# Selective scan with feed-forward: the decay of the GpSimd-made steps moves from PSUM to the SBUF ring

## The reference

```python
dt = jax.nn.softplus(jnp.einsum('blr,dr->bld', x_dbl[..., :DT_RANK], dt_w) + dt_b)
A = -jnp.exp(A_log)
dA = jnp.exp(dt[..., None] * A)
dBu = dt[..., None] * Bm[:, :, None, :] * u[..., None]

def step(h, ins):
    dA_t, dBu_t, C_t = ins
    h = dA_t * h + dBu_t
    y = jnp.einsum('bdn,bn->bd', h, C_t)
    return (h, y)
```

## Time and profile before

| | us |
|---|---|
| median of 3 runs | 493.03 |
| lowest and highest run | 490.91, 496.62 |
| the profiled execution's own time | 496.12 |
| its span | 494.3 |

### The profile page before, as it was taken

The page is one execution under the profiler, slowest core; times in us unless marked ns, Lnnn a source line. Parts: engine busy times, 40 slices in busy tenths (PEclk is TensorE's granted clock), DMA queues, the critical chain, the costliest instruction groups (busy, mean ns, idle before and its releaser), DMA issues. The chain is left out here.

```text
span 494.3 us, 6553 instructions
## 1 busy us (share of the span) xinstructions
PE 410.5 (83%) x2200; PEld 276.7 (56%) x2200; DVE 422.3 (85%) x345; ACT 369.4 (75%) x719; POOL 404.3 (82%) x241
## 2 busy tenths in 40 slices
PE   1947995998699987989898998889998967798854
PEld 0335554664556574555655684555665845457643
DVE  3577997999989998988999879998999989899254
ACT  2298699679966969897889689898789786972040
POOL 1799689797988799988979899989899999958431
PEclk9967999998879998998999899999999895989778
DMA  8251242322241233222232314223322332210001
GB/s 238 87 196 46 86 110 82 110 85 91 64 146 47 90 108 107 86 91 65 85 108 100 112 50 107 86 92 106 108 86 107 79 106 93 70 42 2 0 1 42
DMA packets 17009, 43.48 MB, mean 88 GB/s; under 512 B 1616, under 2 KB 5968, under 8 KB 16976
## 3 DMA queue, kind: packets, MB, share of 16 engines
q1 hardware_dynamic: 16976, 43.06, 27.1%
HBM read 41.48 MB, written 1.57 MB: 87 GB/s over the span
## 5 line engine op out<-in xcount | busy, mean ns | idle before, releaser
L1020 POOL TENSOR_TENSOR hq<-hq,c_tiles 128x1024 f32<-128x1024 f32 x129 | 300.6, 2348 | 45.2 <-DVE hq L1147 42.7
L1147 DVE TENSOR_TENSOR_SCAN hq<-da,bb 128x1024 f32<-128x1024 f32 x113 | 255.9, 2280 | 10.0 <-PE bb L631 2.6
L650 PE MATMUL ysum<-wts,hq 128*128 128x128 f32 x1024 | 150.7, 295 | 18.5 <-POOL hq L1020 17.0
L816 ACT ACTIVATE da<-dt,neg_a 128x511 f32<-128x511 f32 x226 | 147.1, 711 | 7.1 <-DVE hq L1147 6.8
L650 PEld LDWEIGHTS ysum<-wts,hq 128*128 128x128 f32 x1024 | 122.9, 150 | 43.0 <-POOL hq L1020 24.3
L1128 DVE TENSOR_TENSOR bb<-bb,dtu 128x1024 f32<-128x1024 f32 x80 | 97.0, 1213 | 9.3 <-PE bb L604 5.8
L914 ACT ACTIVATE g<-dtu_t,bc_t 128x256 f32<-128x256 f32 x132 | 55.9, 497 | 0.0
L1147 DVE TENSOR_TENSOR_SCAN hq<-bb,dbu 128x1024 f32<-128x1024 f32 x15 | 34.3, 2286 | 13.4 <-ACT bb L827 6.3
L631 PE MATMUL bb<-wts,g 128*128 128x128 f32 x264 | 37.8, 290 | 9.1 <-ACT g L914 7.1
L631 PEld LDWEIGHTS bb<-wts,g 128*128 128x128 f32 x264 | 32.2, 150 | 18.5 <-issue 9.9
L604 PE MATMUL bb<-b_rows,pick 48*128 48x512 bf16 x76 | 30.4, 400 | 9.6 <-DVE hq L1147 9.6
(11 more groups left out here) (127 smaller groups left out, 500.1 us busy)
## 6 DMA issues: line engine op xcount, KB each, us to landing
c_tiles<-bc_rows_dram SPq DMA_DIRECT2D x64, 512.0 KB, 3.6
b_tiles<-bc_rows_dram SPq DMA_DIRECT2D x15, 256.0 KB, 4.4
wconv<-conv_taps_dram SPq DMA_DIRECT2D x2, 512.0 KB, 7.1
x_res<-x_dram SPq DMA_DIRECT2D x1, 768.0 KB, 9.2
out_dram<-o SPq DMA_DIRECT2D x3, 256.0 KB, 2.3
wts<-packed_dram SPq DMA_DIRECT2D x1, 584.0 KB, 10.2
hid<-w_ffn_dram SPq DMA_DIRECT2D x1, 576.0 KB, 8.6
bc_rows_dram<-xdbl SPq DMA_DIRECT2D x8, 64.0 KB, 3.1
```

Source lines behind the costliest of these rows:

```text
L650: mm = nc.tensor.matmul(ysum[:, h, block(b)], hq[:, i % H_RING, h, block(b)], ident, start=(first and b == 0), stop=(i % NS == NS - 1), is ...
L816: ins = nc.scalar.activation(da[:, i % DA_RING, h, 1:SEQ], dt[:, k % 2, h, 1:SEQ], ACT.Exp, scale=neg_a[:, c:c + 1])
L1020: nc.gpsimd.tensor_tensor(hq[:, i % H_RING, halves, :], hq[:, i % H_RING, halves, :], c_tiles[:, n % C_RING, i % 2, :].unsqueeze(1).broadc ...
L1147: nc.vector.tensor_tensor_scan(out=hq[:, i % H_RING].rearrange("p h t -> p (h t)"), data0=decay.rearrange("p h t -> p (h t)"), data1=dbu_t ...
```

## The change

The pooled steps' decay is made like all others, by `exp` into the ring `da`, some five steps ahead. The stage `exp_psum`, its semaphore and its copy of zeros are gone. The pooled scan reads `da` and `dbu`. The bank of `bb` that belongs to a pooled step stays untouched, so the step two later waits for the last scan that did use the bank (`last_in_bank`), which is four before it.

```diff
+def last_in_bank(i):
+
+    return max(n for n in range(i % BB_RING, i, BB_RING) if not is_pooled(n))
...
-        return [("exp", n) for n in ahead.get(i, (i + DA_RING - 1,)) if n < STEPS and not is_pooled(n)]
+        return [("exp", n) for n in ahead.get(i, (i + DA_RING - 1,)) if n < STEPS]
...
-            if i >= 1 and i + 1 < STEPS:
-                order.append(("g_turn" if is_turned(i + 1) else "exp_psum" if is_pooled(i + 1) else "bcast", i + 1))
+            if i >= 1 and i + 1 < STEPS and not is_pooled(i + 1):
+                order.append(("g_turn" if is_turned(i + 1) else "bcast", i + 1))
...
                     if i >= BB_RING:
-                        pe.wait_ge(s_scan, i - BB_RING + 1)
+                        pe.wait_ge(s_scan, last_in_bank(i) + 1)
...
-                elif stage == "exp_psum":
-
-                    i, = a
-                    k, n = i // NS, i % NS
-                    act.wait_ge(s_scan, i - BB_RING + 1)
-                    nc.scalar.activation(bb[:, i % BB_RING, :, 0:1], da[:, 0, :, 0:1], ACT.Copy)
-                    for h in range(2):
-                        c = (2 * (k % 2) + h) * NS + n
-                        ins = nc.scalar.activation(bb[:, i % BB_RING, h, 1:SEQ], dt[:, k % 2, h, 1:SEQ],
-                                                   ACT.Exp, scale=neg_a[:, c:c + 1])
-                    ins.then_inc(s_exp_psum, 1)
...
                     i, = a
+                    dve.wait_ge(s_exp, i + 1)
                     if is_pooled(i):
                         dve.wait_ge(s_dbu_pooled, pooled_steps(i) + 1)
-                        dve.wait_ge(s_exp_psum, pooled_steps(i) + 1)
+                    elif is_turned(i):
+                        dve.wait_ge(s_g_turn, turned_steps(i) + 1)
                     else:
...
-                    decay, dbu_tile = da[:, i % DA_RING], bb[:, i % BB_RING]
-                    if is_pooled(i):
-                        decay, dbu_tile = bb[:, i % BB_RING], dbu
+                    dbu_tile = dbu if is_pooled(i) else bb[:, i % BB_RING]
                     nc.vector.tensor_tensor_scan(out=hq[:, i % H_RING].rearrange("p h t -> p (h t)"),
-                                                 data0=decay.rearrange("p h t -> p (h t)"),
+                                                 data0=da[:, i % DA_RING].rearrange("p h t -> p (h t)"),
                                                  data1=dbu_tile.rearrange("p h t -> p (h t)"), initial=0.0,
```

More of the change, by code:

```diff
@@ L405, in mamba_sandwich @@
         s_exp = sem("da_done")
-        s_exp_psum = sem("da_in_psum_done")
         s_bl = [sem(f"b_tile{n}_loaded") for n in range(POOLED_RING)]
@@ L1132, in _ @@
                     i, = a
+                    dve.wait_ge(s_exp, i + 1)
                     if is_pooled(i):
                         dve.wait_ge(s_dbu_pooled, pooled_steps(i) + 1)
-                        dve.wait_ge(s_exp_psum, pooled_steps(i) + 1)
-                    else:
[L1137 to L1141, removed]
+                    elif is_turned(i):
+                        dve.wait_ge(s_g_turn, turned_steps(i) + 1)
+                    else:
+                        dve.wait_ge(s_dbu, plain_steps(i) + 1)
                     if i >= H_RING:
                         dve.wait_ge(s_fold, i - H_RING + 1)
-                    decay, dbu_tile = da[:, i % DA_RING], bb[:, i % BB_RING]
-                    if is_pooled(i):
-                        decay, dbu_tile = bb[:, i % BB_RING], dbu
+                    dbu_tile = dbu if is_pooled(i) else bb[:, i % BB_RING]
                     nc.vector.tensor_tensor_scan(out=hq[:, i % H_RING].rearrange("p h t -> p (h t)"),
-                                                 data0=decay.rearrange("p h t -> p (h t)"),
+                                                 data0=da[:, i % DA_RING].rearrange("p h t -> p (h t)"),
                                                  data1=dbu_tile.rearrange("p h t -> p (h t)"), initial=0.0,
```

## The result

| | before | changed |
|---|---|---|
| median, us | 494.82 (4 runs) | 509.61 (4 runs) |
| lowest and highest, us | 490.91, 496.89 | 509.15, 510.46 |
| ratio, 95% interval | | 1.031 (1.024 to 1.039) |
| span of the profiled execution, us | 494.3 | 508.7 |

The change made the kernel slower by 14.8 us between the medians. Of the kernel before's 17 executions there, the nine slow ones, more than 1.5% above its fastest, are left out of its median, 492.21 us, and of the ratio, as are eight of 17 beside the other experiments, where its median is 492.55. The difference is +18.7.

The account below looks back on a forecast made before the run. VectorE and GpSimd, both wanting nearly the whole unit, were taken to bound the kernel. Exclusion +14.4, fewer TensorE waits -2.1 and uncovered GpSimd time +1.0 gave +13.3 on 493.0: 506.3 us, range 490 to 518.

Parts of the forecast that it names:

- Exclusion, both ways: Pooled scans with two SBUF inputs and GpSimd operations exclude each other, first come first served; +6 to +22.3 us, chance 0.58.
- The sum over fifteen places: Waits of pooled scans for running GpSimd products, earlier-decay gains included: 5.7 at step 8 plus 8.6 at step 15, +14.4 us.
- Second order: Knock-on effects on VectorE's waits for TensorE and on GpSimd's spare time: -2.1 and +1.0 us.
- waits on TensorE that shrink: A later VectorE waits less for TensorE's broadcasts and turned products: a quarter of 8.4 us, -2.1.
- GpSimd's debt: GpSimd stands still during pooled scans, and its spare time in a unit leaves about 1 us uncovered: +1.0.
- Base: Sum applies to the profiled execution, 496.12 us, 3.1 above the median of the runs; forecast starts from 493.0.
- The earlier decay in front of the Silu: ScalarE's step 8 decay pair precedes the convolution's Silu, hidden by 13.4 us of TensorE waits; counted nothing, at most 9.9 us.
- The earlier release of the bank: Broadcast or turned product two steps after a pooled one no longer waits for its scan; counted nothing, at most 2.0 us.
- GpSimd keeping the port: Rival: GpSimd holds the port across back-to-back instructions; +22.5 us, 515.5 (508 to 524), chance 0.14.
- Only GpSimd waits: Rival: the pooled scan on VectorE never waits; about +1 us, 494 (487 to 501), chance 0.12.
- No exclusion for a scan: Rival: pooled scans overlap GpSimd products undisturbed, so half the earlier starts is kept; -6 us, 487 (481 to 493), chance 0.12.
- Waits that vanish in slack: Rival: VectorE's delays are real but fall into waits on TensorE and tail order; 490 to 497 us, chance 0.04.

Follow-up runs that it names:

- the small kernel: Separate kernel without the reference's computation: eight stages of four VectorE and GpSimd operations, alone or together; two-SBUF scans beside products 17.35 us, scans with one PSUM operand 9.35.
- the kernel with the PSUM operand: Changed kernel, but pooled scans read old values from PSUM as second operand and release the bank as before; 485.15 us, 0.985 of the kernel before.
- the two attempts with a sooner decay: Kernel before with the late decay one slot sooner, operands unchanged: at both steps 490.93 us, ratio 0.999; at step 15 alone 492.39, ratio 1.002.
- the kernel with step 15 alone: The change made only at step 15 of a unit (8 places), step 8 keeping its late decay in PSUM; 514.32 us, 1.046 of the kernel before.
- the small kernel's fifth stage: Stage of the separate two-engine kernel: four VectorE products of two SBUF tiles beside four GpSimd products; 13.40 us.

## Why the prediction was right

The forecast was 506.3 (490 to 518) and slower; measured were 509.6 and +14.8 against +13.3 forecast.

**Exclusion, both ways.** This was taken from one GpSimd instruction of 1.70 us and extended to VectorE without a row. The 4.09 to 4.38 us of eleven pooled scans and the stages of the small kernel show both directions.

**The sum over fifteen places.** Forecast 5.7 at step 8 and 8.6 at step 15. In the changed trace the seven scans at step 8 last 25.1 us instead of 16.0 with 5.3 less idle time before them: +3.9. The eight at step 15 last 32.8 instead of 18.3, less 6.0: +8.5. Together +12.4 of 14.4. The part at step 8 was too large by 1.8. At six of its seven places each turn is shorter than I took it, by about 0.1 (a scan that has waited ends 2.15 us after the product, not 2.29). The seventh, the last unit's, makes 1.3 of the 1.8: I counted +0.07 there, and the trace has -1.2, the scan lasting 2.87 instead of 2.29 us without the 1.79 of idle time before it. GpSimd was behind there and still at the product of step 6 (443.70 to 446.05), so the pooled scan waited for the rest of that one and not for the product of scan 7, which ended at 444.85.

**Second order.** I had -2.1 for waits on TensorE that shrink and +1.0 for GpSimd's debt. Neither is seen in that form: VectorE's other idle time between first and last scan is 23.1 us against 22.6, so nothing was absorbed, and its waits for broadcasts and turned products grew from 8.4 to 9.6. The term that I missed is the end. At the last unit's step 15 I counted -0.01, because the scan would start first. It did; but then the product of the step before waits for it, and nothing after it hides that. Two pieces of the chain of waits at the end, of the kernel before and of the changed one (start, us, what):

```profile
453.59 2.35 POOL hq L1020
...
456.41 2.35 POOL hq L1020
```

```profile
466.42 2.36 POOL hq L1013
...
469.24 4.25 POOL hq L1013
```

The product before the last one lasts 4.25 us on the chain instead of 2.35. From the end of the last scan to the end of the span it was 35.8 us and is 37.3. The balance of the spans closes: +0.45 before the first scan, +12.38 between, +1.55 behind, 14.38. That the forecast of the size came so near is in part luck: step 8 was 1.8 too large, and the end, which I had at nothing, gave nearly as much back; the two terms of the second order, -1.1 together, have nothing that answers to them.

**Base.** I had put the profiled execution 3.1 above the median; with the four runs of each it is 1.3 above, so of the 3.3 us between forecast and median 1.8 are the base and 1.5 the size.

**What was costed at nothing.** The earlier decay in front of the Silu: the Silus wait 9.0 us for TensorE instead of 13.4, and the kernel with the PSUM operand, which has the same order on ScalarE, is faster than before. The earlier release of the bank: the turned products waited 2.0 us for scans before and 0.9 in the changed kernel, no more than I bounded.

**The rivals.** GpSimd keeping the port: refuted by the turns. Only GpSimd waits: refuted by the scans' durations. No exclusion for a scan: refuted; the gain I gave it, -6, is near the 7.4 of the kernel without exclusion. Waits that vanish in slack: refuted for this change. What happened to the two attempts with a sooner decay is akin to it: there the gain went into other waits.

## What to carry to other kernels

Before a tile is moved from PSUM to SBUF, count the SBUF inputs of every VectorE instruction that reads it: with two of them it takes turns with GpSimd instructions that read SBUF, and the one that comes second waits for the rest of the other's instruction, here up to 2.1 us each time (128x1024 fp32). In a profile look for it in the durations, not in the idle time: the same shape in two groups of durations, both engines "busier" with no more instructions. And where several engines are close to the bound, an idle time that is removed in front of one instruction is worth only what the next operand allows; here 12.5 us of it were removed for a gain within the noise. Where two profiles of nearly equal kernels differ in waits for TensorE, compare the granted clock of the same stretch before reading the difference as the change's.

## What was not expected of the hardware

- Two engines that exclude each other alternate strictly when both have work ready: a scan and a product of 128x1024 take 4.28 us a turn, not 2.29 + 2.36 = 4.65.
- The one GpSimd instruction of the earlier trace rows waited for two VectorE instructions in a row, while in the small kernel's fifth stage VectorE's second product waited for GpSimd's first. Why the turn was not taken in the first case no run shows.
- A GpSimd copy beside a scan with two SBUF inputs costs 2.97 us a turn (the scans start at 83.01, 85.99 and 88.96; 12.10 us for four), a memset nothing.
- For 10.20 us at a granted clock of 0.50 TensorE was busy all the time and VectorE waited 3.1 us for its broadcasts (339.50 to 350.81 in the kernel with step 15 alone). At the full clock the same steps of the changed kernel show no such wait.
